# Loading an expert's weights in eight chained pieces of 512 KB instead of four unchained ones of 1024 KB

## The reference, cut to what matters

```python
x = x + gnn(_layernorm(x), src, dst, ...)
# then, on _layernorm(x):
logits = xf @ Wg
topv, topi = jax.lax.top_k(logits, 2)
gate_w = jax.nn.softmax(topv, axis=-1)
h = jax.nn.relu(xf @ W1[e] + b1[e])          # for each expert e
y = h @ W2[e] + b2[e]
y = (y - mean(y)) / jnp.sqrt(var(y) + EPS) * gamma[e] + beta[e]
out = sum over the two chosen experts of gate_w * y     # added to x
```

## Time and profile before

| what | value |
|---|---|
| median of 3 runs | 3008.78 us (3006.24 to 3012.4) |
| the profiled execution, its own time | 3011.95 us |
| its span, first to last instruction | 3009.8 us |
| mean granted TensorE clock | 0.955 of full speed |
| PE, DVE, ACT, POOL busy | 89%, 67%, 48%, 70% |
| the expert stage, from its first transposes to the end | 2256 to 3010 us |
| DMA traffic over the span | 663.25 MB, 220 GB/s |

### The profile page before, as it was taken

One profiled execution on the slowest core, in us unless ns is written; L12 is line 12 of the kernel. 1 busy time (PEld: TensorE's weight loads), 2 busy tenths in 40 slices (PEclk: granted clock), 3 DMA queues, 4 the chain that ended last, 5 costly groups with the idle time before them and its releaser, 6 DMA issues.

```text
span 3009.8 us, 64437 instructions
## 1 busy us (share of the span) xinstructions
PE 2692.4 (89%) x11698; PEld 1974.8 (66%) x11699; DVE 2023.2 (67%) x4826; ACT 1451.8 (48%) x2703; POOL 2094.5 (70%) x2213
## 2 busy tenths in 40 slices
PE   1599999999999997999999999999969999999996
PEld 0476666666676664666666666666647777777875
DVE  7566666666565654877787777787765666666665
ACT  5445444444444443454445444444425555555554
POOL 0777777777777775777777777777725566666665
PEclk9999999999999998999999999999979999999998
DMA  9788889898877776887778787777755555455443
GB/s 362 226 287 294 294 295 294 293 300 285 288 246 226 224 222 216 243 250 241 238 245 250 240 247 244 237 246 237 244 173 134 137 138 128 88 136 139 82 77 67
DMA packets 234585, 663.25 MB, mean 220 GB/s; under 512 B 46616, under 2 KB 48210, under 8 KB 227368
## 3 DMA queue, kind: packets, MB, share of 16 engines
q0 software_dynamic: 151472, 464.79, 54.6%
q10 hardware_dynamic: 62316, 128.09, 12.0%
q1 hardware_dynamic: 20748, 69.89, 6.3%
HBM read 550.93 MB, written 111.69 MB: 220 GB/s over the span
## 4 chain that ended last, share of the span: by engine, by line
POOL 35%; PE 20%; issue 20%; DMA 18%; DVE 2%; POOLq 1%; ACT 1%; SPq 1%; DVEq 1%; ACTq 0%
POOL store_all L685 31%; PE ps L1617 7%; DMA m_g<-gate_scratch,idx_g 5%; DMA out<-store_all,idx_s 4%; PE ps L1643 4%; PE ps L1652 4%; DMA store_all<-h_scratch,srcT 3%; PE ps L1653 3%; DMA store_all<-xn_scratch,srcT 2%; POOL idx_x L698 2%; DMA store_all<-xn_scratch,idx_x 1%; DVE r_lo L1224 1%; POOL store_all L714 1%; DMA xn_scratch<-store_all 1%; PE ps L1708 1%
## 5 line engine op out<-in xcount | busy, mean ns | idle before, releaser
L831 ACT ACTIVATE r_hi<-store_all 128x512 fp32r x1190 | 729.5, 626 | 646.3 <-SPq L569 418.8
L685 POOL DMA_INDIRECT store_all<-xn_scratch,srcT x782 | 807.6, 1033 | 314.7 <-issue 231.0
L685 POOL DMA_INDIRECT store_all<-h_scratch,srcT x782 | 814.8, 1042 | 261.4 <-issue 223.3
L1224 DVE TENSOR_TENSOR r_lo<-store_all,r_hi 128x512 fp32r<-128x512 f32 x1190 | 807.7, 686 | 270.0 <-ACT r_hi L831 267.3
L1652 PE MATMUL ps<-r_hi,sel 128*128 128x512 f32 x1190 | 573.6, 482 | 52.9 <-DVE r_lo L1224 52.7
L1643 PE MATMUL ps<-store_all,sel 128*128 x980 | 536.6, 630 | 0.0
L1653 PE MATMUL ps<-r_lo,sel 128*128 128x512 f32 x1190 | 483.6, 406 | 0.0
L1212 DVE TENSOR_TENSOR sel<-ps,dstT 128x384 fp32r (+4 forms) x602 | 315.5, 524 | 209.1 <-PE ps L1643 136.8
L1617 PE MATMUL ps<-wts,sT 128*128 128x512 f32 x1176 | 410.2, 460 | 0.0
L1617 PE MATMUL ps<-wts,aT 128*128 128x512 f32 x1176 | 374.5, 427 | 0.0
L1617 PE MATMUL ps<-wts,m_hT 128*128 x1224 | 322.0, 413 | 20.9 <-DVE m_hT L1497 19.9
(11 more groups left out here) (274 smaller groups left out, 3337.2 us busy)
## 6 DMA issues: line engine op xcount, KB each, us to landing
expert_weights_scratch<-w_both ACTq DMA_DIRECT2D x64, 512.0 KB
wts<-expert_weights_scratch SPq DMA_DIRECT2D x32, 1024.0 KB, 10.6
store_all<-in_L_ffn_W ACTq DMA_DIRECT2D x64, 256.0 KB
self_t<-xn_scratch ACTq DMA_DIRECT2D x49, 256.0 KB, 6.3
self_t<-h_scratch ACTq DMA_DIRECT2D x49, 256.0 KB
store_all<-in_x ACTq DMA_DIRECT2D x49, 256.0 KB
store_all<-xn_scratch,srcT POOLq DMA_INDIRECT x782, 4.8
store_all<-h_scratch,srcT POOLq DMA_INDIRECT x782, 4.2
```

The costliest lines, as they stand in the source:

```text
L685: pool.indirect_dma_start(rows[:, t % SLOTS, :], None, rows_d, bass.IndirectOffsetOnAxis(ap=srcT[:, t:t + 1], axis=0)).then_inc(s_rows[t % ...
L831: act.activation(r_hi[:, ring(k), :], slot_of(t), ACT.Copy) \
L1224: dve.tensor_tensor(r_lo[:, ring(k), :], slot_of(t), r_hi[:, ring(k), :].bitcast(F32), ALU.subtract).then_inc(S["lo"] if k < ST else S["lo ...
```

## The change

The blocks are loaded in halves: first the high part h = 0 and then the low part h = 1 of each chunk, 512 KB each, with 4 KB in a row for each partition. This holds for all eight experts. For experts 2 to 7, SP also waits after each half until it has landed, before it issues the next one. The three row transfers follow the last half, as before without a wait between them. The semaphore's full count of an expert rises from 7 to 11 times 16.

```diff
-        EXPERT = 16 * (KC + 3)
+        EXPERT = 16 * (2 * KC + 3)
...
-            def load_expert(e, par):
+            def load_expert(e, par, landed=None):
 
                 for k in range(KC):
-                    sp.dma_start(wts_e[:, par, k].bitcast(F32), wsplit_d[e * KC + k] if isinstance(e, int) else
-                                 wsplit_d[bass.ds(e * KC + k, 1)].rearrange("a p h m n -> (a p) h m n")) \
-                        .then_inc(s_expert[par], 16)
+                    for h in range(2):
+                        sp.dma_start(wts_e[:, par, k, h].bitcast(F32), wsplit_d[e * KC + k, :, h] if isinstance(e, int) else
+                                     wsplit_d[bass.ds(e * KC + k, 1), :, h].rearrange("a p m n -> (a p) m n")) \
+                            .then_inc(s_expert[par], 16)
+                        if landed is not None:
+                            alone(sp, s_expert[par], landed + 16 * (2 * k + h + 1))
...
                     alone(sp, M["y"], q + 1)
                     alone(sp, M["out"], q + 1)
-                    load_expert(e, par)
+                    load_expert(e, par, e2 * EXPERT)
                     load_rows_of(e, par)
```

## The result

The changed kernel takes 2995.98 us (median of 7 runs, 2989.66 to 3005.18), the kernel before 3008.78 us (median of 7, 3006.22 to 3016.61). The ratio is 0.9957, with a 95% interval of 0.9945 to 0.997. It is faster by 12.8 us, where 27.8 us were forecast.

What follows compares the result with a forecast made beforehand. The prediction took PE to set the expert stage's pace at 6.64 us a tile, with six loads costing 41.8 us; at 5 x 2.6 + 1 = 14 us they gain 27.8, giving a median of 2981.0 us, range 2968 to 3012.

Steps and rivals of the forecast that it cites:

- Rival 1: Expert stage: delay only spread, extras add up in POOL's in-order queue, loads cost as today; median 3008 us; chance 0.14.
- What the loads cost today: Expert stage: six loads of experts 2 to 7 cost PE 41.8 us, the most the change can win there.
- a load of n tiles costs PE n(e - 0.49) plus what the row transfers add, less 1.2: Expert loads: PE's delay, with e the extra on each scatter; 2.6 us a load, bounds 0 and 7.9.
- what a half adds to a scatter: Scatter beside one chained half: 0.8 us taken, between nothing and the half's own occupation of 1.65 us.
- The row gather: POOL's gather of rows: counted as covered during loads; without that cover at most 2.86 us a load.
- The reserve of 1.2 us: How late a scatter may be before DVE notices: 1.2 us, subtracted once from each load's delay.
- The room of 0.49: POOL's slack in one tile: a 4.8 us scatter allows a 6.15 us period, 0.49 below PE's 6.64.
- The row transfers: Three together after the last half: 2.7 us extra on a scatter, less 0.49 room, 2.2 us a load.
- I price no fall of the clock: PE during loads: stalls come as pieces of a microsecond, so no cost for a lower clock.
- The pitch: SP's time from one chained half to the next: near 4.0 us, bounds 3.5 and 5.1.
- rival 3: Expert 2's load: at a 6 us pitch weights come late, PE waits 5 us once; median 2986; chance 0.05.
- the 49.8 us of room: Time for expert 2's load before PE needs it: 49.8 us against 39 needed, free up to a 5.4 us pitch.

Runs made afterwards that it cites:

- e9: Changed kernel with all loads of experts 2 to 7 left out, so they use old weights and rows; stage loss 5.3 us, one run.
- e11: Changed kernel with the row transfers of experts 2 to 7 left out and the chained halves kept; stage loss 14.8 us, one run.
- e10: Changed kernel with the weights of experts 2 to 7 left out and the three row transfers kept together; stage loss 16.8 us, one run.
- e1: Changed kernel without the waits between the halves of experts 2 to 7; ratio to the kernel before 0.9984, stage loss 37.1 us.
- e14: Changed kernel with whole blocks, experts 3 to 7 one per tile at a scatter's landing, rows chained, expert 2 unchained; ratio to before 0.9942, stage loss 16.1 us.
- e17: Same kernel as e14, run again for times and a second trace; ratio to before 0.9942 for both, stage loss 17.2 us.

## Why the prediction was right and wrong

- **Direction and range: right.** Faster was given 0.74, and 2996.0 lies between 2968 and 3012. The size was wrong, 12.8 us for 27.8, though the forecast's own range of 2971 to 3001 held. The six loads were to cost 14 us and cost 26.8, that is 4.5 us each, inside the bounds of 0 to 7.9 that I had put around 2.6.
- **Rival 1's band** is 3006 to 3018 us by the own time, 6 us to each side of 3011.95, and not 3005 to 3015; nothing rests on it.
- **What the loads cost today: right.** 41.8 us read from PE's timeline, 40.0 measured with e9. The cause was right too: two long scatters a load, through `plus_beta`.
- **The step that failed: "a load of n tiles costs PE n(e - 0.49) plus what the row transfers add, less 1.2".** The term for what a half adds to a scatter was about right: the 32 scatters beside halves alone in the changed kernel's first trace landed 0.5 us late in the mean, where I had 0.8, though the latest by 1.9, beyond my bound of 1.65. Its use was wrong, since this sum knows the scatter alone. The row gather, which I counted as covered, was: PE waited 0.6 us for it in all the loads of the changed kernel. The gates' gather was in no term at all, without a reason given; it took up to 6.8 us from issue to landing beside the row transfers (2788.95 to 2795.8) and gave DVE 16.2 us of waits. The halves were to cost 1.6 us a load, less the reserve, so 0.4; alone they cost 9.5 us in six loads, 1.6 each (e11), and over half of DVE's waits there were for the gates. This is rival 1's mechanism, at part of its strength.
- **The reserve of 1.2 us was credited once a load against everything.** By my terms the rows alone should have cost 1.0 us a load and the halves alone 0.4, 8 us in all with six loads. Alone they cost 11.5 and 9.5 (e10, e11). The reserve was read from one scatter, and for single late scatters it held: in e10 three of them that landed 2.8, 4.6 and 4.6 us late gave DVE waits of 1.7, 3.5 and 3.5 us, 1.1 us less; a fourth, 3.2 late, gave 2.7. The room of 0.49, which I took off as well, was not there beside it. And the reserve says nothing of a delay that reaches DVE through the gates, ahead of `h_lo`.
- **The row transfers: under-priced in their cost, not in the lateness.** With rows alone (e10) the scatters beside them landed at 5.1 to 9.4 us, 2.9 us late in the mean, near the 2.7 taken; two were 4.6 late, beyond my bound of 3.8. Only what exceeds the reserve costs, and a scatter that is not late gives nothing back, so a spread of this size costs more than its mean: DVE's waits were 11.3 us in four loads and none in two. 768 KB of row transfers, three at once, cost as much as 4 MB of chained halves.
- **"I price no fall of the clock": wrong.** Three waits of 1.9 to 3.1 us brought the clock down to 0.62 or 0.63, 1.5 us each. It is not new with the change: five products inside the loads of the kernel before took 4.3 to 5.5 us.
- **SP: half right.** The pitch was 5.0 us and not 4.0, inside the bounds of 3.5 to 5.1. So the load lasted 48 us and not 39, and rival 3, a sign by which I had called the prediction wrong, came true in all three traces, by 1.5, 0.7 and 3.0 us. It came at a pitch below the 5.4 us that I had called free, since the 49.8 us of room were too many. They held the loss of the old load itself: seven periods of 6.635 us are 46.4. In the changed kernel the product was due 2347.94 - 1.46 - 2299.45 = 47.0 us after the first issue. I had taken a half's landing from a load that waited for nothing; with POOL's transfers beside each it was 4.8.
- **The 4 KB rows: at no price, and nothing spoke against it.** e1's loss was no higher than before. The four added issues each for experts 0 and 1 were not tried apart. The stage began 6 us later in the changed kernel's first trace, where I had allowed 4; that execution was 9 us above its median, so one trace does not decide it.
- **The rule on batching** from the Trainium skill, DMA: Bandwidth & Descriptors, section Measured (HBM→SBUF, 128 partitions, SWDGE, issued from GpSimd): the trace agrees that chained halves are slow, 512 KB in 5.0 us, 105 GB/s. By the section Anatomy of one DMA it would have been an estimated 3.2 us; both sections are on transfers that GpSimd issues, and these are issued by SP. As to the stage, e14 and e17 speak neither way: whole blocks, one per tile, gave about the same stage loss in half the tiles, but cost the five placed loads twice what halves did.

## What to carry to other kernels

A background load beside a loop with several small transfers is priced by all the transfers of a tile, not by the one alone that is waited for longest today. One whose wait stands ahead of the critical operation in an in-order queue counts, however small it is. Count for each the room until its wait is felt. And before making a load's pieces smaller, tie each to a moment of the loop: the same halves lost 1 us or less in three loads at one place in the tile, and 3.1 to 5.5 us a load at another. Placed whole blocks lost 2 us a load. Ask also how long the slower load may last for the shortest of its users, and count that room in steady periods, not in a stretch that the old load had lengthened.

## What the hardware showed that I had not expected

The gates' gather moves 128 x 32 bytes, 4 KB. In a steady tile of the kernel before it took 2.4 us, as the chain that ended last shows (start, us, what):

```profile
2340.05 2.40 DMA m_g<-gate_scratch,idx_g
```

Beside the three row transfers of expert 7, issued from 2789.1 on, it took close to 6.8 us. POOL's queue in the changed kernel shows it, from the gather to the index copy that waited for its landing:

```profile
2788.95 0.95 POOL L724 DMA_INDIRECT m_g<-gate_scratch,idx_g  x1 [0.30 <-issue]
...
2795.77 0.18 POOL L706 COPY idx_g<-lstq 128x1 int32 x1 [2.36 <-DMA m_g<-gate_scratch,idx_g]
```

A tiny transfer is not spared by its size. And the row transfers, which read one 2 KB row 128 times over, cost 11.5 us in six loads, as much as the chained halves with five times the bytes (9.5 us; the traces' spread does not tell the two apart). Whether it is their rows of 2 KB, the one source row or that three go at once was not tried apart.
